# The end of a self-attention unit cut into three pieces over three slots, with its multiplication by the reciprocal sums on GpSimd

## The reference

```python
x = x + attn(layernorm(x))               # 32 heads of 32, 8 key/value heads, weights reduced to their signs
x = x + xattn(layernorm(x), ctx)         # 16 heads of 64, keys and values from low-rank products
x = x + ffn(layernorm(x))                # silu(gate) * up, low-rank in and out
```

```python
scores = einsum('bhqd,bhkd->bhqk', q, k) / sqrt(32)
attn = softmax(scores, axis=-1)
out = einsum('bhqk,bhkd->bhqd', attn, v)     # then one more signed linear layer
```

## Time and profile before

| | us |
|---|---|
| median of 3 runs | 1559.61 (1553.19 to 1560.04) |
| the profiled execution, its own time | 1561.65 |
| its span, first to last instruction | 1559.9 |
| PE busy in the span | 1404.1 (90%) |
| DVE busy | 938.7 (60%) |
| ACT busy | 705.4 (45%) |
| POOL busy | 485.2 (31%) |

### The profile page before, as it was taken

The page is one execution under the profiler, slowest core; times in us unless marked ns, Lnnn a source line. Parts: engine busy times, 40 slices in busy tenths (PEclk is TensorE's granted clock), DMA queues, the critical chain, the costliest instruction groups (busy, mean ns, idle before and its releaser), DMA issues.

```text
span 1559.9 us, 22583 instructions
## 1 busy us (share of the span) xinstructions
PE 1404.1 (90%) x8423; PEld 987.5 (63%) x8423; DVE 938.7 (60%) x1643; ACT 705.4 (45%) x1584; POOL 485.2 (31%) x434
## 2 busy tenths in 40 slices
PE   5888899899989998867989889896999999999998
PEld 3555455545554554346767667664788887888886
DVE  5468556845683666456748577474473673673645
ACT  5165603540344045024737557473553453453442
POOL 2036503660455146321112121022352342342331
PEclk9999899999999999879999999997999999999999
DMA  5775645545546433246635445256310210210111
GB/s 189 104 136 115 128 70 123 90 82 108 106 75 102 103 74 79 85 138 168 177 95 149 141 108 158 68 149 207 138 56 1 98 65 0 100 63 0 68 68 54
DMA packets 94880, 157.54 MB, mean 101 GB/s; under 512 B 9910, under 2 KB 49076, under 8 KB 94772
## 3 DMA queue, kind: packets, MB, share of 16 engines
q1 hardware_dynamic: 94772, 156.11, 40.4%
HBM read 82.15 MB, written 25.17 MB: 69 GB/s over the span
## 4 chain that ended last, share of the span: by engine, by line
PE 67%; DVE 13%; DMA 7%; ACT 5%; issue 4%; SPq 3%; POOL 1%; DVEq 0%; ACTq 0%; POOLq 0%
PE bank L930 15%; PE bank L942 7%; PE bank L856 7%; PE bank L737 6%; PE bank L771 3%; PE bank L751 3%; PE bank L915 3%; PE bank L691 3%; DMA q_stack<-hi_lo 3%; PE bank L870 3%; PE bank L784 2%; PE bank L814 2%; PE bank L841 2%; PE bank L955 2%; DVE bn L1182 2%
## 5 line engine op out<-in xcount | busy, mean ns | idle before, releaser
L1460 POOL TENSOR_TENSOR fold<-wide 128x512 f32<-128x512 f32 x128 | 164.0, 1284 | 277.1 <-ACT wide L1010 235.5
L1010 ACT ACTIVATE wide<-bank 128x512 f32<-128x512 f32 x256 | 150.4, 596 | 161.8 <-PE bank L771 159.1
L1263 DVE TENSOR_REDUCE neg_top<-bank 128x2 f32<-128x512 f32 x256 | 171.0, 685 | 55.0 <-PE bank L751 53.2
L1532 POOL TENSOR_TENSOR v_lo<-v_all,v_hi 128x512 fp32r<-128x512 f32 x88 | 122.7, 1395 | 246.7 <-ACT v_hi L1095 246.7
L751 PE MATMUL bank<-k_stack,q_stack 96*128 96x256 f32 x512 | 113.8, 310 | 34.4 <-DVE neg_top L1263 22.4
L771 PE MATMUL bank<-q_stack,k_stack 98*128 98x512 f32 x256 | 141.9, 558 | 2.6 <-ACT wide L1010 2.4
L930 PE MATMUL bank<-pT_hi,v_hi 128*128 128x512 f32 x352 | 137.3, 390 | 2.6 <-POOL v_lo L1532 2.6
L930 PE MATMUL bank<-pT_hi,v_lo 128*128 128x512 f32 x352 | 137.2, 390 | 0.0
L930 PE MATMUL bank<-pT_lo,v_hi 128*128 128x512 f32 x352 | 137.0, 389 | 0.0
L751 PEld LDWEIGHTS bank<-k_stack,q_stack 96*128 96x128 f32 x512 | 97.3, 201 | 62.7 <-issue 23.5
L1417 DVE SCALAR_TENSOR_TENSOR inner<-bank,b_cols,inner 128x512 f32<-128x512 f32 x88 | 65.9, 749 | 112.8 <-PE bank L930 109.4
(11 more groups left out here) (176 smaller groups left out, 3130.1 us busy)
## 6 DMA issues: line engine op xcount, KB each, us to landing
q_stack<-hi_lo SPq DMA_DIRECT2D x96, 256.0 KB, 5.7
xin<-x_scratch SPq DMA_DIRECT2D x33, 512.0 KB, 4.8
xq_stack<-xhi_lo SPq DMA_DIRECT2D x128, 128.0 KB, 2.4
x_res<-in_x SPq DMA_DIRECT2D x22, 512.0 KB, 5.1
x_scratch<-x_res SPq DMA_DIRECT2D x16, 512.0 KB, 2.6
xin<-in_ctx SPq DMA_DIRECT2D x16, 512.0 KB, 4.5
x_group<-x_scratch SPq DMA_DIRECT2D x32, 256.0 KB, 3.4
x_scratch<-x_group SPq DMA_DIRECT2D x32, 256.0 KB, 2.6
```

The lines of the kernel that those rows point to most:

```text
L1010: act.activation(PT[m % PT_RING][:, :], tiles[m % 2][:, :], ACT.Exp).then_inc(sem["tile_exped"], 1)
L1263: dve.tensor_reduce(neg_top[U % 2][:, r, b, :], tops[n % 2][:, :].rearrange("p (a b) -> p a b", a=QT), AX.X, ALU.max, negate=True).then_in ...
L1460: pool.tensor_tensor(fold[f % FOLD_RING][:, :], PT[2 * f % PT_RING][:, :], PT[(2 * f + 1) % PT_RING][:, :], ALU.add).then_inc(sem["folded" ...
L1532: pool.tensor_tensor(lo[:, :, :, 0:n], inner_gu(f, n), hi[:, :, :, 0:n].bitcast(F32), ALU.subtract).then_inc(sem["iw_lo"], 1)
```

## The change

The step `finish` becomes three steps. `sum_turn` has the first turn and the reciprocal on VectorE, `recip_turn` the second turn on VectorE, and `finish` now holds the multiplication, which goes to GpSimd in front of the two instructions that were there. They come at the end of the three slots behind the one that held `finish`: 14, 15 and 16 rather than 13, 22, 23 and 24 rather than 21, and so on. The left-over slots of a group are six rather than two, and they are dealt out anew between the next group's keys and values. The semaphore waits keep their sense; they move with their instructions.

```diff
-        for i in range(GROUP_HEADS + 8):
+        ends = {}
+        for i in range(GROUP_HEADS + 12):
...
                 if i >= 9:
-                    step += [("sums", s - 1)] + ([("finish", (s - 1) // GB)] if (s - 1) % GB else [])
+                    step.append(("sums", s - 1))
+                    if (s - 1) % GB:
+                        for k, piece in enumerate(("sum_turn", "recip_turn", "finish")):
+                            ends[i + 1 + k] = (piece, (s - 1) // GB)
                 if i - 5 < GROUP_HEADS:
                     step += [("mix", s)] + ([("mix_out", s // GB)] if s % GB else [])
+            if i in ends:
+                step.append(ends[i])
...
-            order += key(n, 0) + late[0] + key(n, 1) + late[1] + value(n, 0) + value(n, 1)
+            order += key(n, 0) + late[0] + late[1] + key(n, 1) + late[2] + late[3]
+            order += value(n, 0) + late[4] + value(n, 1) + late[5]
...
-            elif kind == "finish":
+            elif kind == "sum_turn":
                 U = at[0]
...
                     sem["recip"], 1)
+            elif kind == "recip_turn":
+                U = at[0]
                 e.wait_ge(sem["recip"], U + 1)
...
                     sem["recip_set"], 1)
-                e.wait_ge(sem["recip_set"], U + 1)
-                e.wait_ge(sem["mix_copied"], U + 1)
-                e.wait_ge(sem["attn_lo"], U)
-                dve.tensor_tensor(OTn[:, :], OTs_self[:, :], R_sb[:, :], ALU.mult).then_inc(sem["attn_out"], 1)
...
             elif kind == "finish":
                 U = at[0]
                 g, tq = divmod(U, KV_HEADS)
+                e.wait_ge(sem["recip_set"], U + 1)
+                e.wait_ge(sem["mix_copied"], U + 1)
+                e.wait_ge(sem["attn_lo"], U)
+                pool.tensor_tensor(OTn[:, :], OTs_self[:, :], R_sb[:, :], ALU.mult).then_inc(sem["attn_out"], 1)
                 e.wait_ge(sem["attn_out"], U + 1)
```

## The result

| | us |
|---|---|
| the changed kernel, median of 4 runs | 1537.2 (1535.19 to 1539.78) |
| the kernel before, median of 4 runs beside them | 1559.82 (1553.19 to 1563.01) |
| ratio with 95% interval | 0.9861 (0.9834 to 0.9888) |
| profiled execution after: own time, span | 1539.78, 1538.0 |

The forecast was 1530 with a range of 1520 to 1550. The same kernel run again beside the experiments gave 1538.64 and a ratio of 0.9861 as well.

A forecast was written before the change was run, and what follows sets the result against it. TensorE, nearly always busy, was held up by VectorE's bursts (22.4 us behind `neg_top`) and the low clock behind them. -12 - 7 + 2 - 13.5 = -30.5 us from 1561.65 gave 1531, forecast as a 1530 median; range 1520 to 1550, own range 1522 to 1540.

The forecast's parts named there:

- heads of units, nine stalls: First three units of the first three groups: cutting VectorE's burst saves 1.35 us each, 12 us; bounds 9 and 16.
- turns, three: Slots 34 to 41, where the next group's rows are turned: 2.35 us saved three times, 7 us; perhaps only 2.
- clock: Stretches around the stalls: falls to the lower clock go too, returning 80% of 17 us, 13.5; ends 0 and 17.
- ends of three groups: First `o` waits as `recip_turn` stands behind `value`'s evacuation: 2 us lost for three; bounds 0 and 4.
- last group: Chain to 636.43: 0.6 us longer multiplication, but last `fold` no longer queues; nothing, give or take 1.
- The walk through slots 34 to 41: VectorE's queue at the turns: first stall (2.18 us) vanishes, some 0.65 of both is left at slot 41.
- the three stretches of rows 4: Stretches around the stalls with granted clock 0.88, 0.83 and 0.87, said to lose TensorE 17 us.
- a granted share short of 1 times the length is what TensorE loses: Pricing rule for the low-clock stretches: 0.12 x 42 + 0.17 x 30 + 0.13 x 54 = 17 us.
- The rival that the clock stays low: Stalls shrink but clock falls stay or move: -17 us at most, 1543 us; chance 0.15.
- the predicted half microsecond: Wait of `o` for `attnT_lo` between groups, 0.45 us, about 1 after the first group.
- VectorE or the landing hides it: Rival: VectorE's queue catches up no sooner, only the multiplication's time is gained; 1549 to 1553 us; chance 0.10.
- GpSimd becomes the bound: Rival: GpSimd slips, `mix_out` and exponentials wait in each unit, up to 41 us more; 1583 us; chance 0.05.

## Why the prediction was right, and where it was off

**Time.** The median of 1537.2 lies in the forecast's own range, 1522 to 1540, near its upper end. The prediction counted 30.5 us, 22.4 came.

| term | predicted | measured |
|---|---|---|
| heads of units, nine stalls | 12 | 10.9 |
| turns, three | 7 | 3.0 |
| clock | 13.5 | 12.5 |
| ends of three groups | -2 | -3.9 |
| last group | 0 | -0.7 |
| before the units | 0 | 0.7 |

The first two are differences of waits in the two timelines, the clock is what the gains of the three groups' units (6.6 + 9.1 + 10.6 = 26.3) leave after these, and it is set beside the busy time below.

**The heads: right.** The landing of `q_stack` is late next, as the prediction said, with 0.30 to 0.69 us in the second and third group against the 0.35 to 0.45 it worked from. In the first group two heads wait for nothing from the DMA, but 0.75 and 1.05 us for the transposed signs of `signs_o` appeared instead.

**The turns: the step that failed.** The walk through slots 34 to 41 gave 0.65 us of stall at slot 41; it is 2.0 there, with 0.2 more ahead of it, and the gain is 1.0 a group rather than 2.35. The walk, of which the prediction gives only the outcome, let the turns alternate between two banks and overlooked that `top` of slot 41 takes one of them, so that the last turn waits for `hT_lo` of slot 40. In VectorE's timeline that instruction begins at 303.49 and takes 0.67; the turn starts at 304.22. The run with `top` a slot later shows it: the waits for `hT_lo` fell from 5.2 to 0.6 us, and 0.50 us is left of the pair in each group, near the 0.65 of the walk. This term is half of the miss.

**The clock: right in its mechanism, its price per share too high.** By share the three stretches of rows 4 lost 17 us and lose 1.6 now, so 15.4 of 17 were given back rather than 80%. In time it was less. From slot 1 to slot 49 TensorE executes the same matmuls before and after, so its busy time for them can be compared. The sums over these stretches of the first three groups, before and then after:

```profile
sum 223.21, PE 195.70 PEld 121.15 DVE 175.37 ACT 122.01 POOL 123.37; mean PE 65.23 PEld 40.38 DVE 58.46 ACT 40.67 POOL 41.12
```

```profile
sum 196.88, PE 182.92 PEld 114.71 DVE 156.52 ACT 121.44 POOL 136.85; mean PE 60.97 PEld 38.24 DVE 52.17 ACT 40.48 POOL 45.62
```

Busy time fell by 12.8 us, near the 12.5 that the waits leave over. Two things make it less than the share, and how much belongs to each I haven't separated. In the low stretches TensorE was also idle (its busy time in the second stretch of rows 4 is 24.75 of 30 us), and an idle us costs the same at either clock. And between starts the same work took somewhat less than twice as long there. Two projections in the kernel before, at the upper level and then in the low stretch behind the stall of 1.97 us:

```profile
120.36 0.39 PE L737 MATMUL bank<-hT_hi,signs_qkv 128*128 128x512 f16 x1
120.59 0.38 PE L737 MATMUL bank<-hT_lo,signs_qkv 128*128 128x512 f16 x1
...
123.73 0.65 PE L737 MATMUL bank<-hT_hi,signs_qkv 128*128 128x512 f16 x1
124.17 0.63 PE L737 MATMUL bank<-hT_lo,signs_qkv 128*128 128x512 f16 x1
```

Their starts are 0.23 us apart and then 0.44, 1.9 times. So "a granted share short of 1 times the length is what TensorE loses" was an upper bound taken as a value; here some 0.8 of it was lost. The rival that the clock stays low fell. Gaps of 0.3 to 0.7 us once a unit stood at a granted clock of 1.00 in the second and third group; by the rule of the Trainium skill that the prediction weighed (TensorE: Matmul & The Clock Gate, "A second HAM failure mode: psum-queue depth-cycling") they would have kept it swinging, and in this trace they did not.

**The ends of groups: right in place, low in size.** The waits of `o` are the predicted half microsecond (0.73, 0.66, 0.73). The first end cost 2.5 and not 1. Besides the wait of `o`, TensorE's waits for `tmp`, in the stage that prepares the output's scales (below), grew from 4.1 to 4.8 us, and the granted clock there is lower: 0.72 against 0.82 between 180 and 198 us, worth at most 1.8. How the rest splits between the two isn't shown. The prediction costed the order of the steps but did not look at what runs beside them.

**VectorE or the landing hides it: fell.** It would have been 1549 to 1553. **GpSimd becomes the bound:** its mechanism is real, with a price of 1.2 us in the last group's tail and some of its units, and it decides only with 1.3 us more a unit, as the run with two multiplications shows.

**A loose reading.** The prediction says that the VectorE multiplication of 281.97 ended when the `fold` of 281.58 had run. By rows 3 and 6 the `fold` ended at 282.86 and the multiplication at 283.40, 0.54 us later, so most of its own work came after the `fold`. No term rests on this.

**The instruction itself.** The multiplication on GpSimd, ns min, median and max of 32:

```profile
L1483 POOL TENSOR_TENSOR attnT<-attnT_raw,recip_rows x32: 1260/1272/1292, 107.2 to 610.8; 128x512 f32<-128x512 f32 x32
```

It was estimated at 1.28 from `fold`. It took 1.27, and 1.84 times what it took on VectorE (691 ns).

## What to carry to other kernels

When a short burst on one engine stalls another, look up what is late next before pricing its removal: here, in two groups of four, either cutting the burst or moving its longest instruction reached the same floor, the landing of a DMA, so doing both could not bring both gains. When a hand-written order is walked through, write down for every step which ring of buffers it takes from, the rare steps too: one `top` in eight slots turned a wait for two slots back into a wait for one slot back, and moving it by a slot was worth about a third of the whole change. An instruction that is nearly twice as long on an idle engine is a good trade while that engine has room, and the room is to be read from its tightest units, which here were those of the last group.

## What the runs showed of the hardware that I had not expected

A VectorE instruction with a single SBUF input can be held up by GpSimd too. In the changed kernel `recip_turn` of the seventh unit of the first group, at 182.58 us, lets GpSimd's multiplication and halves run beside `tmp` (128x128, reading `ident`). First VectorE, then GpSimd, from the timelines of the changed kernel:

```profile
185.67 1.03 DVE L1216 TENSOR_SCALAR tmp<-ident,channel_scale 128x128 f32<-128x128 f32 x1 [0.77 <-PE bank L709]
```

```profile
185.46 1.15 POOL L1491 TENSOR_TENSOR attnT_lo<-attnT,attnT_hi 128x512 f16<-128x512 f32 x1
```

GpSimd's instruction ended at 186.61 and VectorE's at 186.70. In the kernel before, the same instruction, at 192.72 with GpSimd idle, took 0.28 us. The Trainium skill (SBUF — State Buffer, "Who interferes with whom") counts `tensor_scalar` among the instructions that can take the ports that VectorE shares with GpSimd, and has the later one blocked until the first is done; the trace agrees, with 1.03 against 0.28 us. GpSimd had begun first, by 0.21 us. It is not new with the change: in the kernel before, one `tmp` began at 190.46, 0.05 us behind a `fold`, and took 1.30.

The lower clock does not follow from the size of a single gap. In the changed kernel gaps of 0.3 to 0.7 us, one in some 11 us, left it at 1.00. The gap of 1.51 us at the turns stands in all three groups of seven traces, 21 times, and a fall stands at it 11 times. Of the six gaps of 1.79 to 1.81 us at heads of units in the second and third group of the kernel before, three were followed by a fall (296.92, 419.91 and 447.01) and three were not (271.39, 284.15 and 434.24). What makes the one fall and not the other stays open; no run here was made for it.
